# A scan kernel: TensorE's sums in thirds between the transposes of scan inputs

## The chip, the core and the metric

The kernel runs on one core of a Trainium2 chip. The metric is device time in microseconds (us) for one execution; lower is better. The engines are TensorE (PE, with its weight loads PEld), VectorE (DVE), ScalarE (ACT), GpSimd (POOL) and SyncE (SP), which issues most of the DMAs. Each runs its own instruction stream in order, and they meet only at semaphores.

## The reference

A block on an image of 4 x 32 x 32 tokens with 384 channels: a Mamba-like selective scan in four directions, then a mixture of experts. What matters here is the scan:

```python
def step(h, inp):
    u_t, d_t, B_t, C_t = inp
    dA = jnp.exp(d_t[..., None] * As)
    h = h * dA + (d_t * u_t)[..., None] * B_t[:, :, None, :]
    y = jnp.einsum('bkcn,bkn->bkc', h, C_t)
    return (h, y)
```

There are 192 inner channels, K = 4 directions, N = 16 states and 1024 positions per image. The output of a direction is the sum over the 16 states of state times C; the four directions are then added, normalised, gated and projected, and eight experts (one per token) follow.

## The kernel before, in words

Images are taken in two pairs (`for p in range(PAIRS)`). Of a pair, 128 partitions hold 64 channels of each of two images, and CG = 3 such column groups j make up the 192 channels. A direction is done in two halves of 512 positions, so a pair has 8 **groups** of 16 **steps**; step s handles one state n = s % 16 for all three j. `STEPS` is 128. In the first group of each direction the scans start from zero, in the second from the states that the first kept. Within a step:

- the **input** of the scan, du times the row B of state n, 128 x 3 x 512, is made by one of three makers, by `MAKER = "PDADPDADPDADPDAA"`: GpSimd (P, line 458), VectorE (D, line 898, one step ahead) or ScalarE (A, steps 2, 6, 10, 14, 15). ScalarE makes it from a transposed du with B as a scale per partition (`scale_duT`), and TensorE transposes it back into PSUM (`transpose_input`, line 1249, 12 transposes, four for each j). Before the four for j it waits until the scan two before, counted over all j, is done, since two PSUM banks `dA[0]` and `dA[1]` take turns;
- the **scans**, three on VectorE (line 922), one for each j; each needs its exponentials from ScalarE (line 699, or 694 in A steps);
- the **product** with the row C of state n, one instruction on GpSimd of 128 x 1536 (line 473), in place in a ring slot `X3[c % RING]` (RING = 7). GpSimd also makes the P inputs: in its turn for step s it first makes the input of s + 2, if that is a P step;
- the **sum** over the states: TensorE multiplies the slot by the identity and accumulates in PSUM (`add_up`, line 1223), for each j one matmul of 512 columns, which the profile shows as two instructions. The sum of a step waits for its product (`s_hc`), and frees the ring slot (`s_xfree`). At n = 0 it first opens the accumulation (`open_sums`, line 1213).

TensorE's queue is written out by hand. In its loop over the steps it does the transposes of an A step first, then all sums up to step s - LAG (LAG = 2), except at n = 14, where the transposes of 15 follow at once. After n = 13 it also transposes du for the next group (`transpose_du`, line 1236, 12 transposes). SyncE loads the rows of B and C (line 344), each load waiting for a product or an input of some steps before, and at n = 2 the delta and du of the next group (line 338).

After the loop of a pair TensorE forms means for the layer norm (line 1272), and VectorE subtracts them (line 938); in the first pair VectorE does the statistics of the next pair in between.

Of the kernel before, what the change touches and what calls it, by code (L numbers as in the profile page):

```python
# [13 lines left out]
P = 128  # L14
# [4 lines left out]
CG = 3  # L19
# [17 lines left out]
LAG = 2  # L37
# [13 lines left out]
def build(nc, x, w_in, conv_w, conv_b, w_xd, w_dt, bias_row, a_log, d_skip, ln_g, ln_b, w_out,  # L51
          w_gate, b_gate, w1, w2, w3, sel, ident_d, half_ones, tri_d, out):
    ctx = ExitStack()
    with ctx:
# [1053 lines left out]
        def _(pe):  # L1108
# [15 lines left out]
            for p in range(PAIRS):  # L1124
# [90 lines left out]
                def add_up(s):  # L1215
                    n, c = s % NS, STEPS * p + s
                    if n == 0:
                        if s == 0:
                            pe.wait_ge(s_bt, ND * (p + 1))
                        open_sums(s)  # L1220
                    pe.wait_ge(s_hc, c + 1)
                    for j in range(CG):
                        ins = pe.matmul(bank[j], ident[:, :], X3[c % RING][:, j, :],  # L1223
                                        start=False, stop=(n == NS - 1), skip_group_check=True)
                    ins.then_inc(s_xfree, 1)
# [14 lines left out]
                def transpose_input(s):  # L1240
                    c = STEPS * p + s
                    index = inputs_before(c, "A")
                    pe.wait_ge(s_scaled, 2 * LB * (index + 1))
                    for j in range(CG):
                        e = CG * c + j
                        pe.wait_ge(s_scan, e - 1)
                        for k in range(LB):
                            at = (j * LB + k) * P
                            ins = pe.transpose(dA[e % 2][:, k * P:(k + 1) * P], scaled[index % 2][:, at:at + P],  # L1249
                                               ident[:, :])  # L1250
                        ins.then_inc(s_inT, 1)
# [3 lines left out]
                for s in range(STEPS):  # L1255
                    n, g = s % NS, s // NS
                    if MAKER[n] == "A":
                        transpose_input(s)
                    if not (MAKER[n] == "A" and MAKER[(n + 1) % NS] == "A"):
                        while added <= s - LAG:  # L1260
                            add_up(added)
                            added += 1
                    if n == LAST_D and g + 1 < GROUPS_OF_PAIR:
                        transpose_du(g + 1)
                while added < STEPS:
                    add_up(added)
                    added += 1
# [220 lines left out]
```

## Time and profile before

| | |
|---|---|
| median of 3 runs | 1914.28 us (1909.44 to 1917.96) |
| the profiled execution | 1912.97 us, span 1911.2 us |
| scan loop of the first pair | about 149 to 713 us of the span |
| scan loop of the second pair | about 910 to 1469 us |
| granted TensorE clock, mean | 0.92 of full speed |

A row of the timeline gives the start in us from the span's start, the time from the first start to the last end of the instructions that it merges, the engine, the line, the operation with its tiles, how many there are, and in brackets how long the engine sat idle before and who released it. A merged row hides idle pieces of up to about 0.15 us.

### The profile page before, as it was taken

Reading aid. Unit: us, or ns where it says so; the run is one execution under the profiler, and the core shown is the slowest. Engines: PE = TensorE matmul, PEld = TensorE weight load, DVE = VectorE, ACT = ScalarE, POOL = GpSimd, SP = SyncE. Lnnn points to the kernel's source line nnn. Section 1 sums busy time; section 2 is a strip of 40 time slices with the busy share of each in tenths; the row PEclk is TensorE's granted clock in tenths of the full one; section 3 lists DMA queues with packets and bytes.
Section 4 is the critical chain, followed back from the end, with each engine's and each line's share of the span. In section 5 each row is a group of like instructions: output and inputs, shape, how many; then the busy total and the mean of one; then the engine's idle time right before and its main releaser. Section 6 shows DMA issues by size and latency. Waiting matters only on the chain.

```text
span 1911.2 us, 17753 instructions
## 1 busy us (share of the span) xinstructions
PE 1562.1 (82%) x5004; PEld 776.5 (41%) x5005; DVE 1459.1 (76%) x1570; ACT 1082.1 (57%) x1960; POOL 1309.4 (69%) x501
## 2 busy tenths in 40 slices
PE   5866888887878877986687888888787759999997
PEld 2323433443433434532343443343343335555554
DVE  6588999998999998657999999999996752332332
ACT  3777777776777754377777777777774211111110
POOL 1458999998999991135899999999997122222221
PEclk9877999999999998886899999999999869999999
DMA  3184435326434321228342542443433560111110
GB/s 119 49 304 164 129 109 171 130 96 210 130 102 142 102 90 43 75 79 305 142 130 98 175 134 97 134 140 102 131 106 99 198 258 30 46 46 47 50 50 14
DMA packets 107360, 228.15 MB, mean 119 GB/s; under 512 B 18302, under 2 KB 31137, under 8 KB 103440
## 3 DMA queue, kind: packets, MB, share of 16 engines
q1 hardware_dynamic: 102160, 213.02, 33.7%
q0 software_dynamic: 5120, 14.21, 2.4%
q8 instruction: 33, 0.54, 0.1%
q14 instruction: 47, 0.39, 0.1%
HBM read 184.13 MB, written 44.60 MB: 120 GB/s over the span
## 4 chain that ended last, share of the span: by engine, by line
PE 45%; DVE 21%; POOL 16%; issue 11%; ACT 4%; DMA 1%; SPq 0%; DVEq 0%; POOLq 0%; ACTq 0%
DVE arena L922 14%; POOL arena L473 14%; PE psum L1223 12%; PE psum L1366 10%; PE psum L1385 5%; PE psum L1147 3%; PE psum L1197 3%; DVE arena L898 2%; PE psum L1249 2%; POOL arena L458 2%; PE psum L1294 1%; PE psum L1313 1%; PE psum L1236 1%; PE psum L1159 1%; PE psum L1376 1%
## 5 line engine op out<-in xcount | busy, mean ns | idle before, releaser
L473 POOL TENSOR_TENSOR arena<-arena 128x1536 f32<-128x1536 f32 x256 | 878.2, 3453 | 35.6 <-ACT arena L708 21.6
L1223 PE MATMUL psum<-arena,ident 128*128 128x512 f32 x1536 | 716.6, 617 | 68.4 <-POOL arena L473 68.3
L922 DVE TENSOR_TENSOR_SCAN arena<-psum,arena 128x512 f32<-128x512 f32 x528 | 614.5, 1227 | 0.0
L699 ACT ACTIVATE psum<-arena 128x512 f32<-128x512 f32 x528 | 363.3, 690 | 266.8 <-DVE arena L922 257.5
L1223 PEld LDWEIGHTS psum<-arena,ident 128*128 128x128 f32 x1536 | 295.0, 199 | 455.1 <-issue 325.5
L922 DVE TENSOR_TENSOR_SCAN arena<-arena,psum 128x512 f32<-128x512 f32 x240 | 282.3, 1230 | 38.4 <-PE psum L1249 35.2
L1249 PE MATMUL psum<-ident,arena 128*128 128x128 f32 x960 | 154.3, 294 | 153.0 <-DVE arena L922 152.9
L676 ACT ACTIVATE arena<-arena 128x192 f32<-128x192 f32 x640 | 234.6, 440 | 0.0
L458 POOL TENSOR_TENSOR arena<-arena 128x1536 f32<-128x1536 f32 x64 | 220.6, 3447 | 4.0 <-issue 4.0
L898 DVE TENSOR_TENSOR arena<-psum,arena 128x1536 f32<-128x1536 f32 x112 | 193.8, 1730 | 21.8 <-ACT psum L684 12.2
L1366 PE MATMUL psum<-arena 128*128 x480 | 202.8, 559 | 0.0
L1249 PEld LDWEIGHTS psum<-ident,arena 128*128 128x128 f32 x960 | 112.0, 147 | 211.9 <-DVE arena L922 150.8
L788 ACT ACTIVATE arena<-psum 128x384 f32<-128x384 f32 x40 | 19.6, 490 | 301.6 <-PE psum L1357 301.6
L694 ACT ACTIVATE arena<-arena 128x512 f32<-128x512 f32 x240 | 161.2, 709 | 14.1 <-DVE arena L922 14.1
L510 POOL TENSOR_TENSOR gap<-one 128x1 f32<-128x1 f32 x40 | 11.9, 299 | 211.0 <-DVE arena L1083 211.0
L447 POOL TENSOR_TENSOR arena<-arena 128x1024 f32<-128x1024 f32 x24 | 62.0, 2583 | 100.0 <-DVE arena L885 100.0
L1066 DVE TENSOR_TENSOR arena<-arena,psum 128x469 f32<-128x469 f32 x40 | 25.7, 643 | 123.2 <-ACT arena L793 114.4
L1366 PEld LDWEIGHTS psum<-arena 128*128 128x128 f32 x480 | 88.4, 191 | 77.0 <-issue 66.8
L1385 PE MATMUL psum<-arena 128*128 (+1 forms) x320 | 110.0, 487 | 1.0 <-DVE arena L1073 1.0
L440 POOL TENSOR_TENSOR arena<-arena 128x1024 f32<-128x1024 f32 x16 | 38.0, 2375 | 95.6 <-ACT arena L575 93.6
L880 DVE SCALAR_TENSOR_TENSOR arena<-arena 128x1024 f32<-128x1024 f32 x24 | 44.8, 1865 | 59.6 <-ACT arena L634 59.6
L1197 PE MATMUL psum<-arena 64*128 64x512 f32 x96 | 65.8, 837 | 23.0 <-ACT arena L625 20.3
(160 smaller groups left out, 1474.3 us busy)
## 6 DMA issues: line engine op xcount, KB each, us to landing
arena<-bc_dram SPq DMA_DIRECT2D x864, 128.0 KB, 3.0
step_dram<-arena SPq DMA_DIRECT2D x16, 1536.0 KB, 8.0
arena<-step_dram SPq DMA_DIRECT2D x32, 768.0 KB, 7.8
arena<-in_x SPq DMA_DIRECT2D x8, 1536.0 KB, 9.2
arena<-in_w SPq DMA_DIRECT2D x6, 1876.0 KB, 10.8
t_dram<-arena SPq DMA_DIRECT2D x16, 386.0 KB, 4.0
arena<-in_w SPq DMA_DIRECT2D x4, 1536.0 KB, 12.9
z_dram<-arena SPq DMA_DIRECT2D x2, 1536.0 KB, 5.2
```

Of the source, the lines that this page charges most:

```text
L458: g.tensor_tensor(X3[c % RING], steps[gr % 2][1], Bs[r % B_RING][:, None, :].to_broadcast([P, CG, HALF]), ALU.mult).then_inc(s_dbp, 1)
L473: g.tensor_tensor(x, x, Cs[c % C_RING][:, None, :].to_broadcast([P, CG, HALF]), ALU.mult)\
L676: a.activation(blocks(scaled[index % 2])[:, :, k, b, :], blocks(duT)[:, :, k, b, :], ACT.Copy, scale=BT[:, kk, LB * half + k, b, BY_SCALAR ...
L694: a.activation(dAs[j], steps[g % 2][0][:, j, :], ACT.Exp, scale=A[:, KORDER[kk], j, n:n + 1]).then_inc(s_dAs, 1)
L699: a.activation(dA[e % 2], steps[g % 2][0][:, j, :], ACT.Exp, scale=A[:, KORDER[kk], j, n:n + 1]).then_inc(s_dA, 1)
L898: v.tensor_tensor(X3[c % RING], dups, Bs[r % B_RING][:, None, :].to_broadcast([P, CG, HALF]), ALU.mult).then_inc(s_dbv, 1)
L922: v.tensor_tensor_scan(x, decay, given, 0.0 if first else state[:, n, j:j + 1], ALU.mult, ALU.add).then_inc(s_scan, 1)
L1197: ins = pe.matmul(bank[2 + 2 * j + h], wdt[0:64, KORDER[PREP[i]], j, :], xd[i % 2][0:64, h * HALF:(h + 1) * HALF], start=True, stop=True)
L1223: ins = pe.matmul(bank[j], ident[:, :], X3[c % RING][:, j, :], start=False, stop=(n == NS - 1), skip_group_check=True)
L1249: ins = pe.transpose(dA[e % 2][:, k * P:(k + 1) * P], scaled[index % 2][:, at:at + P], ident[:, :])
L1366: ins = pe.matmul(bk[:, 0:F], xsT[u][:, k, :], w[:, k, bass.ds(e * F, F)], start=(k == 0), stop=(k == KC - 1))
L1385: ins = pe.matmul(bank[6 + u][:, 0:DM], hidT[u][0:m, k, :], W3[0:m, k, bass.ds(e * DM, DM)], start=(k == 0), stop=(k == FC - 1))
```

## The change

`add_up` now takes a piece: a step's sum is split in its three column groups (`piece = 3 s + j`), the wait for the product stands before j = 0 and the ring slot is freed after j = 2. `transpose_input` takes (s, j). In an A step TensorE's queue is now: the four transposes for j = 0, one piece, those for j = 1, one piece, those for j = 2, and a piece too where the next step is also an A step. Pieces go between only up to those of step s - 3, and never one that opens a group. So that they are still there, the step ahead of an A step (n = 5, 9, 13) leaves one step's sum more behind than before. After the transposes the rest up to step s - 2 follows, as before. At n = 2 the order is as before. In steps 6 and 10 the sums of steps 3 and 7 go in between (two pieces, the third follows); in step 14 the three pieces of step 11, and in step 15 two of step 12. The du transposes after n = 13 are no longer preceded by the sum of step 11. The instructions and their number are the same.

```diff
-LAG = 2
@@
-                def add_up(s):
+                def add_up(piece):
+                    s, j = divmod(piece, CG)
                     n, c = s % NS, STEPS * p + s
-                    if n == 0:
-                        if s == 0:
-                            pe.wait_ge(s_bt, ND * (p + 1))
-                        open_sums(s)
-                    pe.wait_ge(s_hc, c + 1)
-                    for j in range(CG):
-                        ins = pe.matmul(bank[j], ident[:, :], X3[c % RING][:, j, :],
-                                        start=False, stop=(n == NS - 1), skip_group_check=True)
-                    ins.then_inc(s_xfree, 1)
+                    if j == 0:
+                        if n == 0:
+                            if s == 0:
+                                pe.wait_ge(s_bt, ND * (p + 1))
+                            open_sums(s)
+                        pe.wait_ge(s_hc, c + 1)
+                    ins = pe.matmul(bank[j], ident[:, :], X3[c % RING][:, j, :],
+                                    start=False, stop=(n == NS - 1), skip_group_check=True)
+                    if j == CG - 1:
+                        ins.then_inc(s_xfree, 1)
@@
-                def transpose_input(s):
+                def transpose_input(s, j):
                     c = STEPS * p + s
-                    index = inputs_before(c, "A")
-                    pe.wait_ge(s_scaled, 2 * LB * (index + 1))
-                    for j in range(CG):
-                        e = CG * c + j
-                        pe.wait_ge(s_scan, e - 1)
...
+                    index, e = inputs_before(c, "A"), CG * c + j
+                    if j == 0:
+                        pe.wait_ge(s_scaled, 2 * LB * (index + 1))
+                    pe.wait_ge(s_scan, e - 1)
...
                 for s in range(STEPS):
                     n, g = s % NS, s // NS
+                    more = MAKER[(n + 1) % NS] == "A"
                     if MAKER[n] == "A":
-                        transpose_input(s)
-                    if not (MAKER[n] == "A" and MAKER[(n + 1) % NS] == "A"):
-                        while added <= s - LAG:
+                        for j in range(CG):
+                            transpose_input(s, j)
+                            if (j < CG - 1 or more) and added < CG * (s - 2) and added % (CG * NS):
+                                add_up(added)
+                                added += 1
+                    if not (MAKER[n] == "A" and more):
+                        behind = 3 if more and n > 2 else 2
+                        while added < CG * (s - behind + 1):
                             add_up(added)
                             added += 1
                     if n == LAST_D and g + 1 < GROUPS_OF_PAIR:
                         transpose_du(g + 1)
-                while added < STEPS:
+                while added < CG * STEPS:
                     add_up(added)
                     added += 1
```

## Rows read from the trace of the kernel before

**Rows 1.** The page, busy time, share of the span and instructions of each engine:

```profile
PE 1562.1 (82%) x5004; PEld 776.5 (41%) x5005; DVE 1459.1 (76%) x1570; ACT 1082.1 (57%) x1960; POOL 1309.4 (69%) x501
```

**Rows 2.** Windows, GpSimd alone: stretch, its length, busy (instructions), clock, DMA share, GB/s:

```profile
188.80:713.50 524.70, 508.84 (x149) 0.95 0.40 127
...
949.90:1468.60 518.70, 508.84 (x149) 0.96 0.38 121
```

**Rows 3.** Waits, VectorE: who was waited for, us in total, times, longest:

```profile
DVE arena L922 <- PE psum L1249: 35.2, 24, 3.7
```

**Rows 4.** Timeline, end of the first group of the first pair:

```profile
199.08 13.67 POOL L473 TENSOR_TENSOR arena<-arena 128x1536 f32<-128x1536 f32 x4
...
201.13 6.78 DVE L922 TENSOR_TENSOR_SCAN arena<-psum,arena 128x512 f32<-128x512 f32 x6
...
202.59 2.84 PE L1223 MATMUL psum<-arena,ident 128*128 128x512 f32 x6 [1.03 <-POOL arena L473]
...
205.99 2.84 PE L1223 MATMUL psum<-arena,ident 128*128 128x512 f32 x6 [0.55 <-POOL arena L473]
...
208.66 1.47 PE L1236 MATMUL psum<-ident,arena 128*128 128x128 f32 x12
...
209.97 1.04 PE L1249 MATMUL psum<-ident,arena 128*128 128x128 f32 x8
...
210.71 6.78 DVE L922 TENSOR_TENSOR_SCAN arena<-arena,psum 128x512 f32<-128x512 f32 x6 [2.79 <-PE psum L1249]
...
211.99 0.66 PE L1249 MATMUL psum<-ident,arena 128*128 128x128 f32 x4 [0.97 <-DVE arena L922]
...
212.70 3.45 POOL L458 TENSOR_TENSOR arena<-arena 128x1536 f32<-128x1536 f32 x1
...
219.05 7.15 DVE L922 TENSOR_TENSOR_SCAN arena<-psum,arena 128x512 f32<-128x512 f32 x6
```

**Rows 5.** Timeline, VectorE, the same place in the last first group:

```profile
1389.55 5.67 DVE L922 TENSOR_TENSOR_SCAN arena<-arena,psum 128x512 f32<-128x512 f32 x5 [3.19 <-PE psum L1249]
```

**Rows 6.** Timeline, a second group:

```profile
240.23 6.98 POOL L473 TENSOR_TENSOR arena<-arena 128x1536 f32<-128x1536 f32 x2 [0.25 <-DVE arena L922]
...
271.52 7.15 DVE L922 TENSOR_TENSOR_SCAN arena<-psum,arena 128x512 f32<-128x512 f32 x6
...
279.60 7.13 DVE L922 TENSOR_TENSOR_SCAN arena<-arena,psum 128x512 f32<-128x512 f32 x6 [0.93 <-ACT arena L694]
```

**Rows 7.** Timeline, TensorE: from transposes to sums, at full clock and at half clock:

```profile
246.50 0.66 PE L1249 MATMUL psum<-ident,arena 128*128 128x128 f32 x4 [1.31 <-DVE arena L922]
...
247.00 5.32 PE L1223 MATMUL psum<-arena,ident 128*128 128x512 f32 x12
...
404.03 1.12 PE L1249 MATMUL psum<-ident,arena 128*128 128x128 f32 x4 [2.18 <-DVE arena L922]
404.94 6.36 PE L1223 MATMUL psum<-arena,ident 128*128 128x512 f32 x12
...
625.55 7.07 PE L1223 MATMUL psum<-arena,ident 128*128 128x512 f32 x12 [2.30 <-POOL arena L473]
```

**Rows 8.** Timeline, loads of steps and rows, GpSimd's waits after late rows, the loop's end:

```profile
231.01 1.22 SPq L338 DMA_DIRECT2D arena<-step_dram  x2
...
243.53 1.73 DVE L898 TENSOR_TENSOR arena<-psum,arena 128x1536 f32<-128x1536 f32 x1
...
328.10 6.86 POOL L473 TENSOR_TENSOR arena<-arena 128x1536 f32<-128x1536 f32 x2 [1.26 <-ACT arena L708]
...
460.74 3.43 POOL L458 TENSOR_TENSOR arena<-arena 128x1536 f32<-128x1536 f32 x1 [4.04 <-issue]
465.23 6.84 POOL L473 TENSOR_TENSOR arena<-arena 128x1536 f32<-128x1536 f32 x2 [1.07 <-ACT arena L708]
473.58 6.85 POOL L473 TENSOR_TENSOR arena<-arena 128x1536 f32<-128x1536 f32 x2 [1.51 <-ACT arena L708]
...
728.37 1.75 DVE L938 TENSOR_TENSOR arena<-arena,psum 128x1536 f32<-128x1536 f32 x1 [0.82 <-PE psum L1272]
```

More of the change, by code:

```diff
@@ L1238, in transpose_du @@
                     ins.then_inc(s_duTps, 1)
-                def transpose_input(s):
+                def transpose_input(s, j):
                     c = STEPS * p + s
-                    index = inputs_before(c, "A")
-                    pe.wait_ge(s_scaled, 2 * LB * (index + 1))
-                    for j in range(CG):
-                        e = CG * c + j
-                        pe.wait_ge(s_scan, e - 1)
[L1247 to L1251, printed above, removed]
+                    index, e = inputs_before(c, "A"), CG * c + j
+                    if j == 0:
+                        pe.wait_ge(s_scaled, 2 * LB * (index + 1))
+                    pe.wait_ge(s_scan, e - 1)
+                    for k in range(LB):
+                        at = (j * LB + k) * P
+                        ins = pe.transpose(dA[e % 2][:, k * P:(k + 1) * P], scaled[index % 2][:, at:at + P],
+                                           ident[:, :])
+                    ins.then_inc(s_inT, 1)
                 transpose_du(0)
```

## The prediction

> **What bounds the kernel now.** I read the page's busy line first [rows 1], then GpSimd's share of the two long stretches in which the scan loop runs [rows 2], then who waited for whom [rows 3], and last the timeline around the steps that the change touches [rows 4 to 8]. GpSimd, 69% busy over the span [rows 1], is busy 508.84 of 524.70 us and 508.84 of 518.70 us within the two loops [rows 2]; VectorE runs its scans back to back except for a few gaps, and most of what it lost there was lost to the input transposes, 35.2 us in 24 places [rows 3]. So the loop has two chains of nearly the same length. In a pair of groups (32 steps) GpSimd has 40 products of about 3.41 us (508.84 / 149), 136.6 us, and a pair takes about 139 to 140 us. TensorE is only a link between them: its queue is in order, so a sum that waits for GpSimd holds the transposes behind it, and these hold VectorE.
>
> The place is steps 13 to 15 of a group. In the first group of a direction, whose scans start from zero (a first group), TensorE was let go by GpSimd's product of step 10 at 202.59 and by that of step 11 at 205.99; then came the 12 transposes of du, and the transposes for step 14 at 209.97, whose result VectorE took at 210.71 after 2.79 us of idleness [rows 4]. All eight first groups have this gap, between 2.52 and 3.70 us, the last of them 3.19 [rows 5]; read off the timeline they sum to 25.8 us. In the groups that go on from kept states (second groups) a scan's pitch is 1.19 us (7.15 / 6) in place of 1.13 (6.78 / 6), VectorE is the slower chain, and the same place costs 0.93 us [rows 6]; six of the eight have such a gap, 6.2 us together. There GpSimd idles in small pieces, as the 0.25 us before 240.23 [rows 6], because VectorE came out of the first group late. **That GpSimd idleness is what can be won**: 524.70 - 508.84 = 15.9 us in the first loop, of which 1.26 + 4.04 + 1.07 + 1.51 = 7.9 us follow late rows of B [rows 8] that the change doesn't touch, so 8.0; and 518.70 - 508.84 = 9.9 in the second. The ceiling is 17.9 us. By pitch instead of busy time the ceiling is higher: four GpSimd products take 212.70 - 199.08 = 13.62 us from start to start [rows 4], so 149 need 149 x 3.405 = 507.3, which gives 9.5 + 11.4 = 21 us.
>
> **The change part by part.** No instruction is added or removed; only TensorE's order changes, in four of a group's five transposed steps (6, 10, 14, 15). At step 2 nothing changes, since the sum of the step before has the old place there.
>
> *Steps 6 and 10.* The sum of step 3 (or 7) stood ahead of the transposes; its thirds now stand behind each third of these. VectorE makes an input for the next step before it scans step 6 (1.65 us from start to start), so that the second third of the transposes has over 2 us of slack and the third one waits for the first scan anyway. A third of a sum, two instructions at 0.43 us = 0.86 us (12 in 5.32 us [rows 7]), fits. I cost this at nothing; if that cover were gone it would be the 0.23 us per third worked out below. The new dependence, that the second transposes of step 6 stand behind GpSimd's product of step 3, is looser than the old one, under which all of them did.
>
> *Step 14, its head.* The sum of step 11 leaves the place ahead of the du transposes. The transposes of step 14 can then start after the product of step 10, its sum (6 x 0.43 = 2.58) and the du transposes (209.97 - 208.66 = 1.31): 202.59 + 2.58 + 1.31 = 206.5. They must also wait for the second scan of step 13, which ends near 206.9 (201.13 + 4 x 1.13 + 1.22). The third scan ends at 207.9, and 0.74 us pass from the transposes to the scan (209.97 to 210.71 [rows 4]): 206.9 + 0.74 = 207.7, in time. The gap of 2.79 is gone. In groups in which GpSimd is further behind, the gain is the distance of two products, 205.99 - 202.59 = 3.40 us, which leaves 0 to 0.3 of the others. In second groups the sum that goes away (2.58) is longer than the gap, which goes too. The du transposes, now 3.4 us or less earlier, have their operands by then: the step loads of a group are issued some fifteen steps ahead, and the last VectorE input that reads the old du is that of step 13, made before 201.13. Saved on VectorE: 25.8 + 6.2, less some 0.5 that stays, about 31.5 us.
>
> *Steps 14 and 15, the new cost.* Here VectorE scans six times with no other work, and its pitch of 1.13 sets a pace: a third of the transposes may start only once the scan two before is done, and must be ready when the one before it ends. In the kernel before, the transposes that follow the first scan of step 14 start at 211.99 and the third scan is due at 210.71 + 2 x 1.13 = 212.97, so slack is 212.97 - 211.99 - 0.74 = 0.24 us. Now there is a piece of a sum between every two: 0.50 us from the start of four transposes to the piece (246.50 to 247.00) plus 0.86 is a cycle of 1.36 [rows 7]. Five pieces lie between the first and the last transposes of the two steps, each 0.23 longer than a scan: 1.15 us, less 0.24 of slack where the first was not late, so 0.9 to 1.15. In second groups 5 x (1.36 - 1.19) = 0.85, less a slack of about 0.3 (two pitches longer by 0.06 each, less a slightly longer scan), 0.55. Over all: 8 x 1.05 + 8 x 0.55 = 12.8 us on VectorE. The bounds of this cost: 0 if a piece overlaps the tail of the transposes completely, and the half-clock price below if not.
>
> *Sum on VectorE*: 31.5 - 12.8 = 19 us. *Ceiling by GpSimd*: 17.9 to 21. The two chains then are within 0.3 us of each other per pair of groups, and two such chains joined by short buffers don't both run without a pause. I take off 0.8 for the second pair of the second loop, where VectorE waits for B rows again, and about 3.2 for two groups in which the sum of step 10 falls on a half clock: after 2.30 us of idleness 12 instructions took 7.07 instead of 5.32 us [rows 7]. 17.9 - 4 = 14 us. What is late next is GpSimd itself: VectorE, once ahead, is stopped at step 16, whose input GpSimd makes after its product of step 13.
>
> *Who waits behind the new waits.* Behind TensorE's wait for the product of step 12, now within step 15, stand the last two thirds of that step's transposes. It is not late: that product comes 6.8 us after that of step 10, the piece and the transposes add 0.86 + 0.74, so the scan may start at 8.4 after it, while the pace above brings VectorE there at 4.6 + 4 x 1.36 = 10.0. The ring slots of x are freed by up to one step later, and the earliest to need one is seven steps on. The SyncE queue is driven by GpSimd's products and shifts with them. The gain of the first loop reaches its end: VectorE's statistics and TensorE's mean end there within 0.82 us of each other [rows 8], and both start earlier.
>
> **A rule weighed.** In the rows, pieces of TensorE work of 0.63 to 0.66 us with 0.4 to 1.0 us of idleness between them kept the full clock (2.4 GHz) all through steps 14 and 15 (0.66 at 211.99 [rows 4]); half clock (1.2 GHz) is seen behind single gaps as those of 2.18 and 2.30 us [rows 7]. The Trainium skill, "TensorE: Matmul & The Clock Gate", section "A second HAM failure mode: psum-queue depth-cycling", says that frequent micro-idles between groups of matmuls that cycle through PSUM banks make the clock swing between its levels; the change cuts dense sums into such groups. By that rule the slow rival below would be the forecast; the trace so far speaks for the other.
>
> **The rivals.**
> 1. *VectorE's lead is lost again* (B rows for step 7 late, or a string slower than 1.36 per cycle). For it: SyncE issues the step loads at 231.01, the B rows behind them, and VectorE uses these at 243.53 [rows 8]; in second groups it would now ask for them about 2 us earlier (2.79 - 0.9), and where more loads are under way they were late already. Against it: in first groups it asks as early already without a stall outside of those loads. Half a microsecond per group, 16 x 0.5 = 8 us, leaves 6 of 14: 1906 to 1908.
> 2. *GpSimd's chain isn't eased*: the gaps close, but VectorE is held at the same distance by GpSimd's input of step 16, and GpSimd's idle pieces stay. It gives 1911 to 1914. Against it: that input is done at 212.70 + 3.45 = 216.15, while VectorE reached step 16 only at 219.05 [rows 4]; with 2.79 less and 0.9 more it comes at 217.2, still after it.
> 3. *Half clock in the strings, slower.* At 1.2 GHz the piece takes 1.72, and 0.91 us lie between transposes and piece (404.03 to 404.94 [rows 7]): a cycle of 2.6, five of which cost 5 x (2.6 - 1.16) = 7.2 us in a group. If all 16 groups did this it would cost 115 us against 31.5 saved, a time near 1997. Each such group costs 6.4 more than I count, so it decides from the third of the 16 on, and five would give 1914 - 14 + 5 x 6.4 = 1932.
>
> **How the numbers follow.** The profiled execution took 1912.97 us (span 1911.2), 1.3 below the median of 1914.28. 1912.97 - 14 = 1899; for the median 1914.28 - 14 = 1900. Chances: this forecast (gain 10 to 21) 0.60; rival 1 0.23; rival 2 0.10; rival 3 0.07. The range reaches from the ceiling, 1914 - 21 = 1893, to within rival 2, 1911. 0.5% is 9.6 us, about what a measurement of this kernel can tell from no change: faster 0.60, same 0.33, slower 0.07.
>
> **What would show it.** Right: in first groups no gap of over 1 us before the scans of step 14, and the six scans of steps 14 and 15 in 7.7 to 8.0 instead of 6.78 us; GpSimd's idleness in the two loops down from 25.7 to about 12; VectorE's waits for the input transposes many and short, of 0.2 us. Wrong: transposes of 1.1 us within the strings (rival 3), waits of the D input for B rows in groups 1, 3 and 5 (rival 1), GpSimd idling as before (rival 2).

## The result and the profile after

| | before | changed |
|---|---|---|
| median of 6 runs each | 1912.62 us (1909.44 to 1917.96) | 1897.72 us (1892.87 to 1901.21) |
| ratio, 95% interval | | 0.9921 [0.9898, 0.9943] |
| profiled execution | 1912.97, span 1911.2 | 1899.25, span 1897.4 |

The change makes the kernel 0.8% faster, 15 us; the two profiled executions differ by 13.7. Two single executions of the runs below, one of the kernel before (4548.76 us) and one of a variant (3149.66 us), fell in a slow state and count in no median or ratio. The changed kernel's page, its busy time by engine, answers [rows 1]:

```profile
PE 1552.7 (82%) x5004; PEld 767.2 (40%) x5005; DVE 1463.4 (77%) x1570; ACT 1081.1 (57%) x1960; POOL 1306.8 (69%) x501
```

The windows of the two loops, GpSimd alone, as in [rows 2] (the program counts 150 operations here and 149 there, as the end of one reaches into the stretch):

```profile
188.10:706.70 518.60, 507.76 (x150) 0.95 0.41 128
...
945.60:1457.60 512.00, 507.76 (x150) 0.96 0.39 123
```

GpSimd's idleness in the two stretches fell from 25.8 to 10.8 + 4.2 = 15.1 us, by 10.7. Its busy time fell too, from 508.84 to 507.76 us in each, for the same work; why was not tried. VectorE's wait for the input transposes, [rows 3], from 35.2 to 15.3:

```profile
DVE arena L921 <- PE psum L1249: 15.3, 14, 1.9
```

The timeline at the end of the first group of the first pair, to be held against [rows 4]:

```profile
201.84 4.54 PE L1223 MATMUL psum<-arena,ident 128*128 128x512 f32 x6 [2.21 <-POOL arena L472]
...
206.21 1.47 PE L1237 MATMUL psum<-ident,arena 128*128 128x128 f32 x12
...
207.52 0.60 PE L1249 MATMUL psum<-ident,arena 128*128 128x128 f32 x4
...
207.96 1.02 PE L1223 MATMUL psum<-arena,ident 128*128 128x512 f32 x2
...
208.26 7.68 DVE L921 TENSOR_TENSOR_SCAN arena<-arena,psum 128x512 f32<-128x512 f32 x6 [1.43 <-PE psum L1249]
...
208.82 0.60 PE L1249 MATMUL psum<-ident,arena 128*128 128x128 f32 x4
```

Only the sum of step 10 (two instructions for each j, x6) stands ahead of the du transposes, and the thirds (x2) go between the transposes (x4), start to start 208.82 - 207.52 = 1.30 us. The gap ahead of step 14 is 1.43 in place of 2.79, and the six scans take 7.68 in place of 6.78. The sum of step 10 took 4.54 us, not 2.84: after 2.21 us of idleness it began at half clock (the granted clock from 201.84 to 206.21 was 0.61 of full speed). In the second group, as in [rows 6], there is no gap and the six scans take 7.56:

```profile
276.82 7.56 DVE L921 TENSOR_TENSOR_SCAN arena<-arena,psum 128x512 f32<-128x512 f32 x6
```

The length of a scan loop is read as from the start of GpSimd's first product to the end of its last. For the second pair, two rows of before and then two of the changed kernel:

```profile
915.19 6.84 POOL L473 TENSOR_TENSOR arena<-arena 128x1536 f32<-128x1536 f32 x2 [6.42 <-ACT arena L708]
...
1465.13 3.42 POOL L473 TENSOR_TENSOR arena<-arena 128x1536 f32<-128x1536 f32 x1 [0.30 <-DVE arena L922]
```

```profile
911.71 6.84 POOL L472 TENSOR_TENSOR arena<-arena 128x1536 f32<-128x1536 f32 x2 [6.41 <-ACT arena L707]
...
1450.18 3.45 POOL L472 TENSOR_TENSOR arena<-arena 128x1536 f32<-128x1536 f32 x1 [1.82 <-DVE arena L921]
1454.07 3.43 POOL L472 TENSOR_TENSOR arena<-arena 128x1536 f32<-128x1536 f32 x1 [0.44 <-DVE arena L921]
```

1468.55 - 915.19 = 553.4 us before, 1457.50 - 911.71 = 545.8 after: 7.6 us less. The first pair's loop went from 559.2 to 552.5, 6.7 less. The two make 14.2. The span is 13.8 shorter, as the stretch between the loops is 3.3 us longer (205.1 for 201.8) and what follows the second 2.8 shorter. The first loop has waits for late rows of B which vary from kernel to kernel (VectorE waits 1.85 and 6.95 us before, 0.39 and 7.31 after; the profile names no releaser for them, the code waits for a B row there). The second has little of that (0.83 and 1.20), so its length is the yardstick below. It is read from one execution of each kernel. The changed kernel, profiled twice, gave 545.8 and 545.4.

### The profile page after: what moved, and what is told of

The parts are those of the page before. It is cut to its first block, busy times and chain, and to the rows that moved or that the text cites. A ratio compares the mean times of both kernels' runs of the same rounds, so it can differ in the third digit from the quotient of the medians.

```text
span 1897.4 us, 17753 instructions
## 1 busy us (share of the span) xinstructions
PE 1552.7 (82%) x5004; PEld 767.2 (40%) x5005; DVE 1463.4 (77%) x1570; ACT 1081.1 (57%) x1960; POOL 1306.8 (69%) x501
## 4 chain that ended last, share of the span: by engine, by line
PE 35%; DVE 26%; POOL 18%; issue 14%; ACT 4%; DMA 2%; SPq 1%; DVEq 0%; POOLq 0%; ACTq 0%
DVE arena L921 17%; POOL arena L472 16%; PE psum L1372 10%; PE psum L1391 5%; DVE arena L897 4%; PE psum L1146 3%; PE psum L1223 3%; PE psum L1196 3%; POOL arena L457 2%; PE psum L1300 1%; PE psum L1249 1%; PE psum L1319 1%; DMA arena<-bc_dram 1%; PE psum L1158 1%; PE psum L1382 1%
## 5 line engine op out<-in xcount | busy, mean ns | idle before, releaser
L1223 PE MATMUL psum<-arena,ident 128*128 128x512 f32 x1536 | 743.0, 620 | 72.7 <-POOL arena L472 72.7
L1223 PEld LDWEIGHTS psum<-arena,ident 128*128 128x128 f32 x1536 | 283.0, 198 | 386.8 <-issue 258.9
L921 DVE TENSOR_TENSOR_SCAN arena<-arena,psum 128x512 f32<-128x512 f32 x240 | 288.5, 1240 | 20.0 <-PE psum L1249 15.3
L1249 PEld LDWEIGHTS psum<-ident,arena 128*128 128x128 f32 x960 | 117.7, 146 | 271.2 <-issue 132.9
L897 DVE TENSOR_TENSOR arena<-psum,arena 128x1536 f32<-128x1536 f32 x112 | 194.4, 1736 | 21.1 <-ACT psum L683 12.2
L693 ACT ACTIVATE arena<-arena 128x512 f32<-128x512 f32 x240 | 160.3, 709 | 11.5 <-DVE arena L921 10.8
## 6 DMA issues: line engine op xcount, KB each, us to landing
arena<-in_w SPq DMA_DIRECT2D x6, 1876.0 KB, 10.7
```

The source lines that it names most:

```text
L693: a.activation(dAs[j], steps[g % 2][0][:, j, :], ACT.Exp, scale=A[:, KORDER[kk], j, n:n + 1]).then_inc(s_dAs, 1)
L897: v.tensor_tensor(X3[c % RING], dups, Bs[r % B_RING][:, None, :].to_broadcast([P, CG, HALF]), ALU.mult).then_inc(s_dbv, 1)
L921: v.tensor_tensor_scan(x, decay, given, 0.0 if first else state[:, n, j:j + 1], ALU.mult, ALU.add).then_inc(s_scan, 1)
```

## The experiments

Here is what was measured; both loops are those of the profiled execution, in us.

| kernel | median us | ratio to before, 95% | first loop | second loop |
|---|---|---|---|---|
| before | | 1 | 559.2 | 553.4 |
| changed | 1897.72 | 0.9921 [0.9898, 0.9943] | 552.5 | 545.8 |
| changed, again | 1899.94 | 0.9931 [0.9902, 0.9959] | 553.3 | 545.4 |
| steps 6 and 10 only | 1909.18 | 0.9969 [0.9952, 0.9987] | 558.8 | 550.2 |
| steps 14 and 15 only | 1902.23 | 0.9936 [0.9912, 0.9959] | 559.6 | 545.3 |
| sum of 11 put off whole | 1915.56 | 0.9999 [0.9977, 1.0021] | 561.0 | 551.4 |
| sum of 10 held too | 1918.09 | 1.0014 [0.9994, 1.0034] | 564.8 | 556.7 |
| idleness filled | 1903.12 | 0.9932 [0.9901, 0.9963] | 556.1 | 545.4 |
| last group in the old order | 1895.62 | 0.9890 [0.9846, 0.9933] | 557.0 | 543.7 |
| step 2 as well | 1914.15 | 1.0003 [0.9977, 1.0028] | 560.6 | 555.6 |
| light input of step 8, old order | 1910.54 | 0.9954 [0.9935, 0.9974] | 559.0 | 552.5 |
| light input of step 8, new order | 1903.32 | 0.9920 [0.9892, 0.9948] | 560.1 | 546.3 |
| light input of step 12, old order | 1897.69 | 0.9899 [0.9869, 0.9930] | 550.0 | 543.5 |
| light input of step 12, new order | 1902.42 | 0.9943 [0.9918, 0.9967] | 558.2 | 548.8 |

Medians of different rows weren't all taken together; each ratio is against the kernel before, run beside it on the same chip. A loop and a median need not agree: in these fourteen profiled executions the stretch between the loops took 201.3 to 208.6 us and what follows the second loop 436.1 to 443.7, and the changed kernel alone had 205.1 and 201.4 between them.

### Each half of the change alone

```diff
-if (j < CG - 1 or more) and added < CG * (s - 2) and added % (CG * NS):
+if (j < CG - 1 or more) and added < CG * (s - 2) and added % (CG * NS) and n < 14:
...
-behind = 3 if more and n > 2 else 2
+behind = 3 if more and 2 < n < 13 else 2
```

> Only steps 6 and 10 have the new order; steps 13 to 15 are as in the kernel before. Theory A (the gain comes from the head of step 14, where the sum of step 11 went away): the gaps of 2.5 to 3.7 us ahead of step 14 in the first groups stay, and the time is within 2 us of before, 1911 to 1914. Theory B (the gain comes from having thirds between transposes wherever that is done, steps 6 and 10 being half of the places): about half of the 15 us, 1904 to 1907.

The other half has `n >= 14` and `3 if n == 13` in these places.

> Only steps 14 and 15 have the new order; steps 6 and 10 are as before. Theory A: all but 0 to 2 us of the gain, 1897 to 1900. Theory B: half of it, 1904 to 1907.

Steps 14 and 15 give all of the second loop's gain (545.3) and nothing in the first loop of that execution (559.6), where VectorE waited 4.05 and 10.15 us for late B rows, against 1.85 and 6.95 before. The ratio, 0.9936, shows most of the gain. Steps 6 and 10 alone give 3.2 us of the second loop and a ratio of 0.9969, which is more than theory A's "within 2 us" (about 6 us); the interval, 2.5 to 9 us, does not shut out theory B's half. In that kernel the gaps at step 14 grew where the waits ahead of them went: the timeline of VectorE in the kernel with steps 6 and 10 alone has 4.00 us there in the first group of the second loop (3.53 before):

```profile
971.36 6.78 DVE L921 TENSOR_TENSOR_SCAN arena<-arena,psum 128x512 f32<-128x512 f32 x6 [4.00 <-PE psum L1249]
```

In the kernel before VectorE also waited 0.8 to 1.0 us at step 6 or 10 of some first groups, as here:

```profile
937.16 3.44 DVE L922 TENSOR_TENSOR_SCAN arena<-arena,psum 128x512 f32<-128x512 f32 x3 [1.04 <-PE psum L1249]
```

With the sum of step 3 or 7 out of the way this is gone, VectorE comes earlier, and part of what it won it loses at step 14. The two halves don't add up, 3.2 + 8.1 is more than 7.6, as GpSimd's chain leaves little more to win: in the changed kernel it idles 4.1 us in the whole second loop (busy 541.65 of 545.79), 2.3 of them at its very end.

### The sum of step 11 put off, without thirds

```diff
-if (j < CG - 1 or more) and added < CG * (s - 2) and added % (CG * NS):
+if (j < CG - 1 or more) and added < CG * (s - 2) and added % (CG * NS) and n < 14:
```

> As the changed kernel, but no thirds go between the transposes of steps 14 and 15: the sum of step 11 is put off whole, to behind the transposes of step 15. Theory A (what helps is that the sum of step 11 isn't ahead of the transposes; the thirds between them only cost): the six scans of steps 14 and 15 take 6.8 and 7.2 us instead of 7.68 and 7.56, the head gap of about 1.5 us stays, VectorE gains some 9 us over the kernel, of which GpSimd's nearly full chain lets through 0 to 4: 1894 to 1898. Theory C (the thirds are needed, because three sums in a row behind step 15 free the ring slots too late): slower than the changed kernel, 1900 or more, with new waits of VectorE or GpSimd at the inputs of the next group.

Theory C's end came about, though not by ring slots. The scans of steps 14 and 15 take 6.8 to 6.9 us in the first groups, as expected; what is lost is lost at step 2 of the next group. The timeline of this kernel where the first group of the first loop passes into the second (TensorE, then VectorE at step 2), and VectorE's row at step 2 one group later:

```profile
212.40 13.04 PE L1223 MATMUL psum<-arena,ident 128*128 128x512 f32 x30
225.28 1.04 PE L1249 MATMUL psum<-ident,arena 128*128 128x128 f32 x8
...
226.01 3.62 DVE L921 TENSOR_TENSOR_SCAN arena<-arena,psum 128x512 f32<-128x512 f32 x3 [1.58 <-PE psum L1249]
...
298.16 3.44 DVE L921 TENSOR_TENSOR_SCAN arena<-arena,psum 128x512 f32<-128x512 f32 x3 [3.89 <-PE psum L1249]
```

Thirty instructions, the sums of steps 11 to 15, run from 212.40 with no pause until the transposes of step 2, and VectorE waits for these 1.58 us here and 3.89 in the next group. It was TensorE's own work, not GpSimd's product, that came last. Every group but the first of a loop has such a wait, of 1.43 to 3.93 us; in the changed kernel one in each loop has one. The changed kernel does five of those fifteen thirds between the transposes, in time that TensorE otherwise spends waiting for scans. So the thirds pay for the deferral: without them it is worth nothing, 0.9999.

### One step further behind

```diff
-if (j < CG - 1 or more) and added < CG * (s - 2) and added % (CG * NS):
+if (j < CG - 1 or more) and added < CG * (s - (3 if n >= 14 else 2)) and added % (CG * NS):
...
-behind = 3 if more and n > 2 else 2
+behind = {12: 3, 13: 4}.get(n, 3 if more and n > 2 else 2)
```

> As the changed kernel, but steps 14 and 15 trail by one step more: the sum of step 10 too is held back and goes in thirds between the transposes of step 14, that of step 11 between those of step 15. Theory D (what still holds the head of step 14, 1.4 to 1.9 us, is only that the transposes stand behind the sum of step 10): the gap goes, and the time is 1893 to 1897. Theory E (TensorE's clock: without that sum it is idle for over 4 us ahead of the du transposes and of step 14, so that the transposes and thirds of steps 14 and 15 run at 1.2 GHz, a cycle of up to 2.6 us in place of 1.30 for part of the six scans): the six scans take 9 us or more, and the time is 1905 or more.

Both happened, and theory E decides. The gap in front of step 14 is gone (0.19 us), and there are new ones inside. The timeline, rows of TensorE and VectorE, at step 14 of the third group of the second loop (a first group):

```profile
1115.00 1.02 PE L1249 MATMUL psum<-ident,arena 128*128 128x128 f32 x4 [4.09 <-DVE arena L921]
1115.82 1.91 PE L1223 MATMUL psum<-arena,ident 128*128 128x512 f32 x2
1116.15 1.22 DVE L921 TENSOR_TENSOR_SCAN arena<-arena,psum 128x512 f32<-128x512 f32 x1 [0.19 <-PE psum L1249]
...
1117.52 1.06 PE L1249 MATMUL psum<-ident,arena 128*128 128x128 f32 x4
...
1118.68 1.22 DVE L921 TENSOR_TENSOR_SCAN arena<-arena,psum 128x512 f32<-128x512 f32 x1 [1.31 <-PE psum L1249]
```

After 4.09 us of idleness the transposes take 1.02 and a third 1.91 (0.60 and 1.02 in the changed kernel): a cycle of 2.52 us, near the 2.6 of the slow rival. The granted clock from 1115.00 to 1118.60 was 0.53 of full speed, and one or two cycles per group pass before it is full again. In most first groups this only replaces the gap of 1.4 us; in second groups, which had none, it adds 1.25 + 1.24 in the first loop's first one, and 1.25 + 0.80, 1.25 + 0.75 and 1.25 + 1.18 in three of the second loop's. These three make 6.5 of the 10.9 us by which the second loop is longer than the changed kernel's. The last group, which ran at half clock already, adds a wait of 1.23 at step 10.

### The half clock at the sum of step 10

```diff
...
+                    if n == 11:
+                        for _ in range(8):
+                            pe.matmul(bank[0][:, 0:P], zero[:, :], ident[:, :], start=False, stop=False,
+                                      skip_group_check=True)
                     if n == LAST_D and g + 1 < GROUPS_OF_PAIR:
...
```

The tile `zero` is set to zeros by GpSimd at the start of the kernel.

> The changed kernel with 8 matmuls more of 128 columns in TensorE's queue after the sum of step 9 of each group, with a weight of zeros, so that they add nothing to the sums; they fill 1.8 us of the 2 to 3 us in which TensorE waits for GpSimd's product of step 10. Theory H (the gap of 1.4 to 1.9 us that is left ahead of step 14 is the sum of step 10 at 1.2 GHz, 4.3 to 4.5 us instead of 2.84, after that idleness): the sum takes 2.84, the gap falls to 0 to 0.3, the time by 0 to 3 us, 1894 to 1898, since GpSimd has little idleness left. Rival: the sum of step 10 is held by its product alone; gap and time stay, or grow where the filling is itself late.

TensorE and VectorE in a first group of this kernel; the row with the zero weight is the filling:

```profile
1227.83 1.95 PE L1273 MATMUL psum<-ident,zero 128*128 128x128 f32 x16
1230.89 2.84 PE L1225 MATMUL psum<-arena,ident 128*128 128x512 f32 x6 [1.11 <-POOL arena L474]
...
1235.61 7.68 DVE L923 TENSOR_TENSOR_SCAN arena<-arena,psum 128x512 f32<-128x512 f32 x6 [0.42 <-PE psum L1251]
```

The sum takes 2.84, the gap in that group falls from 1.74 to 0.42, and in the four first groups of the loop from 1.43, 0, 1.74 and 1.86 to 0, 0, 0.42 and 0.38. The half clock was the cause of nearly all of it. Theory H had the time at 1894 to 1898 us; it was 1903.12, ratio 0.9932, against 0.9921 and 0.9931 of the changed kernel. The loop is not shorter either, 545.4. What VectorE gains at step 14 it now loses at step 2, where it waits 1.89, 0.79, 1.90 and 1.08 us in four groups of the second loop, and 1.59 in one group of the changed kernel's. TensorE and VectorE at the first of these:

```profile
974.68 7.11 PE L1225 MATMUL psum<-arena,ident 128*128 128x512 f32 x12 [2.46 <-POOL arena L474]
...
982.37 3.62 DVE L923 TENSOR_TENSOR_SCAN arena<-arena,psum 128x512 f32<-128x512 f32 x3 [1.89 <-PE psum L1251]
```

TensorE waits there for a product, and the sums that follow, partly at half clock, stand ahead of the transposes of step 2. GpSimd is busy 541.66 of 545.43 us, so its chain leaves VectorE next to nothing more to win.

The length of the idleness alone does not tell whether the clock falls. The sum of step 10 of the seventh group of the first loop, in the two profiled executions of the changed kernel:

```profile
618.88 4.33 PE L1223 MATMUL psum<-arena,ident 128*128 128x512 f32 x6 [2.81 <-POOL arena L472]
```

```profile
620.10 2.84 PE L1223 MATMUL psum<-arena,ident 128*128 128x512 f32 x6 [2.82 <-POOL arena L472]
```

### Lighter GpSimd work, in two places

In `input_of` of GpSimd, for n == 8 and then for n == 12 instead, in both orders of TensorE:

```diff
-                    g.tensor_tensor(X3[c % RING], steps[gr % 2][1], Bs[r % B_RING][:, None, :].to_broadcast([P, CG, HALF]),
-                                    ALU.mult).then_inc(s_dbp, 1)
+                    w = 8 if n == 8 else HALF
+                    g.tensor_tensor(X3[c % RING][:, :, 0:w], steps[gr % 2][1][:, :, 0:w],
+                                    Bs[r % B_RING][:, None, 0:w].to_broadcast([P, CG, w]), ALU.mult).then_inc(s_dbp, 1)
```

> The kernel before with less GpSimd work: at step 8 of every group GpSimd makes only 8 of the 512 columns of the scan's input (the rest of that input is left as it lies), which takes some 3.3 of 68 us from its chain in each group, so that it no longer sets the pace. Theory F (the gaps ahead of step 14 are GpSimd's lateness carried through TensorE's queue): the gaps of 2.5 to 3.7 us shrink to under 0.5, and the time falls by about 30 us, to 1880 to 1887. Rival G (the gaps are TensorE's own work in that place, 2.6 us of sum and 1.3 us of du transposes, whatever GpSimd does): the gaps stay, 1905 or more.

> The changed kernel with the same lighter GpSimd work (8 of 512 columns of the input of step 8). Theory F: there is nothing left to win at the head of step 14 in either order, and the new order's thirds between the transposes still slow the six scans of steps 14 and 15 (7.68 for 6.78, 7.56 for 7.15), 8 x 0.9 + 8 x 0.4 = 10 us: slower than the light kernel of the old order by 5 to 12 us. Rival G: faster than it by about 15 us, as with full GpSimd work.

Theory F fell. GpSimd lost 25 us of work per loop, the gaps of the old order stayed (2.79 to 3.70 us) and so did its loops, 559.0 and 552.5. Rival G's range came true, yet not for its reason, as the same edit at step 12 shows. Of the two light kernels the new order is the faster, by 7 us in the medians, where F had it slower and G had it faster by 15.

Where the 25 us went is seen in GpSimd's timeline from the light input on, in the third group of the second loop (a first group, old order):

```profile
1085.28 0.24 POOL L459 TENSOR_TENSOR arena<-arena 128x24 f32<-128x24 f32 x1
1088.19 6.85 POOL L474 TENSOR_TENSOR arena<-arena 128x1536 f32<-128x1536 f32 x2 [2.67 <-ACT arena L709]
1096.54 6.86 POOL L474 TENSOR_TENSOR arena<-arena 128x1536 f32<-128x1536 f32 x2 [1.50 <-ACT arena L709]
1103.33 3.46 POOL L459 TENSOR_TENSOR arena<-arena 128x1536 f32<-128x1536 f32 x1
```

GpSimd, ahead now, waits 2.67 + 1.50 us for ScalarE, whose copy of a kept state (line 709) waits for that step's scans. That is more than the 3.2 us it was spared. The input of step 12 (at 1103.33) and the products of steps 10 and 11 then come as late behind VectorE as before.

The time is a little better than the loops say: the ratio of the old order, 0.9954, is clear of 1 and worth 5 to 12 us. The profiled execution, 1915.08 us, is the slowest of its eight (the others took 1903.37 to 1912.51), and where those gained is not shown.

> The kernel before, with GpSimd's input of step 12 (not that of step 8) cut to 8 of 512 columns, the rest left as it lies. That input stands in GpSimd's queue between the products of steps 9 and 10, so that here the products of steps 10 and 11, for which TensorE waits ahead of step 14, come some 3.3 us earlier. Theory F2 (the gaps ahead of step 14 are made by the run of product 9, input 12, products 10 and 11 in GpSimd's queue, and lightening it elsewhere was no use because GpSimd then only waited for scans): the gaps fall to under 0.8 us, and the second loop from 553 to 538 to 544 us, the time to 1885 to 1897. Rival G (TensorE's own sum and du transposes in that place): the gaps stay over 2 us, time 1905 to 1913.

> The changed kernel with the same lighter input of step 12. Under F2 the new order has nothing to win at the head of step 14 any more and still pays for the thirds (7.68 for 6.78 and 7.56 for 7.15 us in the six scans), but it keeps what steps 6 and 10 gave (some 3 us of a loop): second loop within 3 us of that of the light kernel of the old order, on either side, where the full kernels differ by 7.6. Under G it is shorter by 7 us as before.

In the kernel of the old order with the light input of step 12 the gaps are 0.95 us in all first groups (under 0.8 was expected) and none in second ones. Its loops are 9.2 and 9.9 us shorter than those of before, and its median is 1897.69. GpSimd, TensorE and VectorE in one of them:

```profile
1225.28 0.27 POOL L459 TENSOR_TENSOR arena<-arena 128x24 f32<-128x24 f32 x1
...
1227.36 6.84 POOL L474 TENSOR_TENSOR arena<-arena 128x1536 f32<-128x1536 f32 x2 [1.81 <-ACT arena L709]
...
1230.86 2.84 PE L1224 MATMUL psum<-arena,ident 128*128 128x512 f32 x6 [0.87 <-POOL arena L474]
...
1231.25 6.78 DVE L923 TENSOR_TENSOR_SCAN arena<-psum,arena 128x512 f32<-128x512 f32 x6
...
1234.26 2.84 PE L1224 MATMUL psum<-arena,ident 128*128 128x512 f32 x6 [0.56 <-POOL arena L474]
...
1238.98 5.67 DVE L923 TENSOR_TENSOR_SCAN arena<-arena,psum 128x512 f32<-128x512 f32 x5 [0.95 <-PE psum L1250]
```

The input of step 12 takes 0.27 us here; TensorE gets the product of step 10 at 1230.86, 0.39 us ahead of the scans of step 12, and that of step 11 3.01 behind their start. In [rows 4] these came 1.46 and 4.86 behind it. So F2 holds: what made the gap was the run of product 9, input 12, products 10 and 11 in GpSimd's queue, each 3.4 us, and not how much GpSimd has to do in a group. And where that is gone the new order's loops are longer: 558.2 and 548.8, 8.2 and 5.3 us more than the old one's (I had allowed 3). Whether the time is longer too is not shown: the ratios, 0.9943 and 0.9899, have intervals that overlap, and the two profiled executions differ by 1.2 us only. The thirds still take their 0.9 and 0.4 us, and some strings begin at half clock: in five of the eight groups of the new order's second loop VectorE waits 0.88 to 1.26 us, or 0.79 and 0.72, within one.

### The last group, and step 2

```diff
-if (j < CG - 1 or more) and added < CG * (s - 2) and added % (CG * NS):
+if (j < CG - 1 or more) and added < CG * (s - 2) and added % (CG * NS) and (n < 14 or g < GROUPS_OF_PAIR - 1):
...
-behind = 3 if more and n > 2 else 2
+behind = 3 if more and n > 2 and (n < 13 or g < GROUPS_OF_PAIR - 1) else 2
```

> The changed kernel, but the last group of each pair has the old order in steps 13 to 15. In the changed kernel TensorE is idle for 3 us ahead of step 14 there, the first transposes and thirds run at 1.2 GHz, and GpSimd waits 1.82 + 0.44 us for the last two scans, where it waited 0.41 + 0.27 before. If that is a cost of the new order: these waits fall back to about 0.7, and the time by 2 x 1.6 = 3 us, 1893 to 1896. If not (the lateness comes with VectorE from the groups ahead): the waits stay and the time too, 1896 to 1899.

In the changed kernel the last group has no du transposes and no sum of step 11 ahead of step 14. TensorE's timeline there shows idleness and then half clock:

```profile
1443.73 0.63 PE L1249 MATMUL psum<-ident,arena 128*128 128x128 f32 x4 [2.99 <-DVE arena L921]
1444.20 1.59 PE L1223 MATMUL psum<-arena,ident 128*128 128x512 f32 x2
1445.58 1.06 PE L1249 MATMUL psum<-ident,arena 128*128 128x128 f32 x4
```

GpSimd then waits 1.82 + 0.44 us at the loop's end (rows above). In the old order VectorE's six scans of that group take 7.14 us with no gap, and GpSimd's last products run on in one row:

```profile
1435.71 21.03 POOL L472 TENSOR_TENSOR arena<-arena 128x1536 f32<-128x1536 f32 x6
```

The second loop is 543.7, 2.1 and 1.7 us shorter than the changed kernel's two. The median, 1895.62, and the ratio, 0.9890, are the best of all kernels that do the whole work, but the interval [0.9846, 0.9933] doesn't set it apart from the changed kernel. The first loop, 557.0, is longer than the changed kernel's, with 10.77 us of waiting for a B row at one place. The profiled execution took 1896.11 us, the changed kernel's two 1899.25 and 1896.03.

The next kernel has this and `behind = 3` at n = 1 as well:

> The changed kernel with two more edits: the last group of a pair has the old order in steps 13 to 15 (as in the run before of that name), and step 2 gets the new order as well: the sum of step 15 of the group before is held back at step 1 and goes between the transposes of step 2. The aim is VectorE's waits of 1.6 us at step 2, which the new order shows in one of eight groups a loop and the variants more often. If the sum of step 15 ahead of these transposes is their cause: they go, second loop 541 to 544 us, time 1890 to 1896. If opening the next group's sums later costs as much (they wait for ScalarE, which waits for that sum): no gain over the last-group variant, 1895 to 1899, with later transposes of step 6.

It lost the whole gain, 1.0003, second loop 555.6, which neither branch of the expectation had (1890 to 1896 or 1895 to 1899). The waits at step 2 went, and VectorE's waits for ScalarE's exponentials came, 28.1 us in 14 places. ScalarE and VectorE at steps 2 and 3 of a second group:

```profile
1133.29 2.80 ACT L719 ACTIVATE arena<-psum 128x512 f32<-128x512 f32 x3 [3.51 <-PE psum L1223]
1135.88 1.28 ACT L698 ACTIVATE psum<-arena 128x512 f32<-128x512 f32 x2
...
1136.71 3.63 DVE L921 TENSOR_TENSOR_SCAN arena<-psum,arena 128x512 f32<-128x512 f32 x3 [2.68 <-ACT psum L698]
```

At step 2 ScalarE copies the finished sums of the group before out of PSUM (line 719), and waits for the last of them. Put behind the transposes of step 2, the sum of step 15 holds ScalarE for 3.51 us, the exponentials of step 3 stand behind it, and VectorE waits 2.68 us for them. Against the kernel with the last group in the old order (0.9890, second loop 543.7), from which it differs in this alone, it is 11.9 us longer in the second loop. So the old order at step 2, which the changed kernel keeps, is needed.

> The changed kernel as it is, beside the others on the same chip, as the measure for them: 1894 to 1901 by the runs so far.

1899.94 us, as expected.

## Why the prediction came out right, point by point

**The time.** Forecast 1900 for the median and 14 us of gain; measured 1897.7 and 14.9, in the profiled executions 13.7. The forecast held, but not by the sum as written: that it came so close is partly luck. The 14 us were to be idleness of GpSimd; 10.7 of them were, another 2.2 came from GpSimd's operations being shorter, which nobody forecast, and the rest before the stretches begin. On VectorE the 31.5 us to be saved at step 14 were 22.2 (gaps of 32.0 us before, 9.8 after), against which stand the thirds, 12.2 us longer in the sixteen groups (12.8 said), new waits at step 2 (1.57 + 1.59) and waits at steps 6 and 10 that went (3.75).

**The place.** Right: the head of step 14 gave the gain, as the run with steps 14 and 15 alone shows.

**Whose lateness it was.** Here a step was wrong in part. I took GpSimd's idleness in the loop for what can be won, as if its chain had to be full. The light input of step 8 shows that GpSimd's total isn't what bounds the loops before: with 25 us less to do, they were 0.2 and 0.9 us shorter. The bound is a local one, four GpSimd operations in a row between the scans of step 9 and the sum of step 11, which TensorE's queue turned into a wait of VectorE. In the changed kernel the ceiling does show: GpSimd idles 4.1 us in the second loop, and with the half clock removed VectorE's gaps moved to step 2 and the loop didn't change. The kernel of the new order with the light input of step 8 isn't shorter either (546.3), though GpSimd idles 29.2 us in it (busy 517.08 of 546.29). So VectorE's chain with its waits is about as long as GpSimd's, as the sum had them, 19 against 17.9 to 21.

**Steps 6 and 10, "cost at nothing".** The cost is small at most: no wait of over 0.6 us at steps 6 and 10 is left in the changed kernel. But the new order also removes waits of 0.8 to 1.0 us that I had not counted; alone they give 3.2 us of the second loop.

**The head of step 14.** Mis-sized. I expected the gap to fall to under 0.3 us, but for two groups with a half clock. It stayed at 1.4 to 1.9 in six of the eight first groups, each with 2.2 to 2.9 us of idleness ahead of the sum of step 10, and that sum began at 1.2 GHz (4.3 to 4.5 us). In the other two the idleness was 1.9 us, the sum took 2.84 and there was no gap. The cause was named, its frequency was not: two groups were said. It cost the time nothing that shows, by the run with the idleness filled.

**The string.** Right: a cycle of 1.30 (1.36 said), six scans in 7.68 (7.7 to 8.0 said) and 7.56 (7.7). What I had wrong is their role: I wrote them down as a new cost. Putting the sum off without thirds is worth nothing.

**Who waits behind the new waits.** Right for the product of step 12: no new wait for it shows. Missed: the transposes of step 2, late by 1.57 and 1.59 us in one group of each loop. And VectorE's waits for input transposes were to become many and short; they are 14, the longest 1.9 us.

**The rivals.** Late B rows cost the changed kernel no more than before (7.7 us in the first loop, 8.8 before; 1.2 and 0.8 in the second), but in other profiled executions of the new order more: 10.3 us of the first loop in the changed kernel again, 14.2 with steps 14 and 15 only. GpSimd's input of step 16 shows in no wait of VectorE. The half clock in the strings did occur, in the last group of each pair (2.3 us of GpSimd's idleness where there was 0.7 before), and it was the fate of the variant that waits longer ahead of step 14; in the changed kernel the sum of step 10 and the du transposes stand right ahead of the string, and in the other fourteen groups it runs at full clock. As to the rule of the Trainium skill on micro-idles ("TensorE: Matmul & The Clock Gate", section "A second HAM failure mode: psum-queue depth-cycling"): the section speaks of micro-idles between groups of matmuls. In these fourteen groups the strings of steps 14 and 15 hardly idle at all (0.60 to 0.63 us for the transposes and 1.02 for the thirds), so the trace neither bears the rule out nor refutes it. Where a string of the changed kernel did fall to half clock, a single gap of 2.48 to 3.10 us stood before it, as in steps 14 and 15 of the last group (2.99 us) or in step 10 of some second groups (2.50 us at 1289.73).

**GpSimd's idleness** fell to 15.1 us, 12 said: about 2.3 us in each last group that I did not foresee.

Open: why the waits for late B rows in the first loop vary so (6.95 to 10.77 us at one place), and why GpSimd's operations are shorter in the new order, wasn't tried.

## What to carry to other kernels

When an engine with an in-order queue links two others, look for the item in its queue that waits longest for one of them ahead of work that the other needs, and move that item behind; but give it a place in time in which the engine waits anyway, or its work only comes back as a backlog at the next meeting point (here: 0.9999 without the thirds). Lightening an engine tells where its lateness matters only if it is done at the right place in its queue: the same 25 us less took 0.9 us off the second loop at one step and 9.9 at another. Before sums are held back, look at who reads the finished ones.

## What the runs showed of the hardware

Holding work back has a price on TensorE through its clock. After gaps of 2.2 to 2.9 us the sum of step 10 took 4.3 to 4.5 us in place of 2.84 in six groups of the changed kernel, and after one of 4.09 transposes took 1.02 in place of 0.60. Not every such gap has the price: with 2.81 us of idleness the sum took 4.33 in one execution, and with 2.82 it took 2.84 in another of the same kernel (granted clock 1.00); with the sum of step 11 put off whole, four sums after 2.19 to 2.23 us took 2.84, and three after 2.21 to 2.25 took 4.54. Eight matmuls with a weight of zeros in such a gap, leaving at most 1.11 us of it, brought every one of these sums back to 2.84 or less.

Within a string that alternates four transposes with two 512-column instructions, start to start is 1.30 us, where I took 1.36 from the rows of before: the third of a sum starts 0.44 us after the transposes, and 0.50 where these had to wait for a scan.
